# Recurrent attention: the bias of half the heads' decays subtracted on VectorE, their exponentials taken in one instruction

## The reference

```
logfg = log_sigmoid(f_pre); Fcum = cumsum(logfg)
Dmat  = Fcum[s] - Fcum[t] + i_pre[t]          (causal, -inf above the diagonal)
m     = max_t Dmat;  Smat = exp(Dmat - m)
C     = (q k^T / sqrt(dqk)) * Smat
n     = max(|sum_t C|, exp(-m));  h = (C / n) v
```

## Time and profile before

| | |
|---|---|
| median of 3 runs | 699.81 us (698.16 to 700.64) |
| the profiled execution, its own time | 699.76 us |
| its span in the profile | 698.0 us, 12153 instructions |
| TensorE busy | 672.2 us (96%) |
| VectorE busy | 517.6 us (74%) |
| ScalarE busy | 371.4 us (53%) |
| GpSimd busy | 131.0 us (19%) |

### The profile page before, as it was taken

How to read it: one execution, slowest core, us unless ns; L and a number is a source line. 1 busy time by engine, 2 the same in 40 slices (tenths; PEclk the granted TensorE clock), 3 DMA queues, 4 the chain that set the end, 5 groups by cost and what they waited for, 6 DMA issues and landing times.

```text
span 698.0 us, 12153 instructions
## 1 busy us (share of the span) xinstructions
PE 672.2 (96%) x4808; PEld 563.1 (81%) x4808; DVE 517.6 (74%) x919; ACT 371.4 (53%) x775; POOL 131.0 (19%) x125
## 2 busy tenths in 40 slices
PE   7998998999999999999999999999899999999997
PEld 7866875778787888878888878887787889889886
DVE  7736678887957576566675575757679998989996
ACT  5886878856634444444353442446565454454541
POOL 7144535410000020000200002000123213203220
PEclk8999999999999999999999999999999999999999
DMA  5088452000100001010001100150000000000000
GB/s 196 5 253 291 118 157 72 2 1 0 63 1 31 0 1 60 3 31 1 1 23 40 31 1 0 51 223 2 0 1 1 0 10 23 1 31 1 1 31 31
DMA packets 24008, 31.27 MB, mean 45 GB/s; under 512 B 1232, under 2 KB 19952, under 8 KB 23184
## 3 DMA queue, kind: packets, MB, share of 16 engines
q1 hardware_dynamic: 23296, 29.18, 13.1%
q10 hardware_dynamic: 656, 1.31, 0.5%
HBM read 28.18 MB, written 2.31 MB: 44 GB/s over the span
## 4 chain that ended last, share of the span: by engine, by line
PE 68%; DVE 20%; ACT 7%; issue 3%; POOL 1%; DMA 1%; DVEq 0%
PE bank L89 21%; PE bank L91 20%; PE bank L90 20%; DVE l_ring_lo L2535 3%; DVE l_ge L2516 2%; DVE l_h L2531 2%; DVE l_o L2539 1%; DVE h_raw L1214 1%; DVE l_h L2488 1%; ACT m_W L703 1%; PE bank L513 1%; DVE h_ring_lo L1219 1%; PE bank L486 1%; PE bank L501 1%; DVE l_oT_lo L2545 1%
## 5 line engine op out<-in xcount | busy, mean ns | idle before, releaser
L1214 DVE TENSOR_TENSOR h_raw<-h_s,bank 128x512 f32<-128x512 f32 x104 | 71.5, 687 | 107.5 <-ACT h_s L1204 93.2
L1204 ACT ACTIVATE h_s<-bank 128x512 f32<-128x512 f32 x104 | 62.2, 598 | 164.0 <-PE bank L91 163.8
L1219 DVE TENSOR_TENSOR h_ring_lo<-h_raw,h_ring_hi 128x512 fp32r<-128x512 f32 x92 | 69.0, 750 | 0.1
L1208 ACT ACTIVATE h_ring_hi<-h_raw 128x512 fp32r<-128x512 f32 x104 | 64.8, 623 | 2.3 <-DVE h_raw L1214 2.3
L90 PE MATMUL bank<-fused_lo,h_ring_hi 128*128 128x256 f32 x208 | 58.4, 281 | 0.0
L2235 ACT ACTIVATE l_s<-bank 128x512 f32<-128x512 f32 x32 | 19.1, 598 | 64.6 <-PE bank L91 64.6
L89 PE MATMUL bank<-l_xT_hi,l_wgu 128*128 128x512 f32 x128 | 51.3, 401 | 0.1
L89 PE MATMUL bank<-f_yT_hi,mlp_hi 128*128 128x512 f32 x128 | 50.7, 396 | 0.2 <-DVE f_yT_lo L1327 0.2
L90 PE MATMUL bank<-l_xT_lo,l_wgu 128*128 128x512 f32 x128 | 50.3, 393 | 0.0
L91 PE MATMUL bank<-l_xT_hi,l_lo 128*128 128x512 f32 x128 | 50.2, 393 | 0.0
L91 PE MATMUL bank<-f_yT_hi,fused_lo 128*128 128x512 f32 x128 | 50.0, 390 | 0.0
(11 more groups left out here) (372 smaller groups left out, 1977.8 us busy)
## 6 DMA issues: line engine op xcount, KB each, us to landing
m_W<-m_scratch SPq DMA_DIRECT2D x16, 512.0 KB, 6.5
fused_raw<-in_fused SPq DMA_DIRECT2D x1, 3584.0 KB, 13.4
res<-in_x SPq DMA_DIRECT2D x4, 512.0 KB, 6.1
fused_raw<-in_fused SPq DMA_DIRECT2D x2, 1024.0 KB, 9.0
f_mask<-expert_weights SPq DMA_DIRECT2D x8, 256.0 KB
l_raw<-in_layer SPq DMA_DIRECT2D x1, 2048.0 KB, 8.8
out_x<-res SPq DMA_DIRECT2D x16, 128.0 KB, 1.9
f_xw<-in_turned_x SPq DMA_DIRECT2D x3, 512.0 KB, 5.8
```

Source lines behind the costliest of these rows:

```text
L1204: self.nc.scalar.activation(self.s[u % 2][r, :], gate[r, :], ACT.Silu).then_inc(self.silu.sem, 1)
L1208: self.nc.scalar.activation(self.unit(i, u)[0], self.product(i, u), ACT.Copy).then_inc(self.hi.sem, 1)
L1214: self.nc.vector.tensor_tensor(out=self.product(i, u), in0=self.s[u % 2][r, :], in1=up[r, :], op=ALU.mult).then_inc(self.hidden.sem, 1)
L1219: self.nc.vector.tensor_tensor(out=lo, in0=self.product(i, u), in1=f32(hi), op=ALU.subtract).then_inc(self.lo.sem, 1)
```

## The change

The bias of four of the eight heads (SHARED = 4, heads 4 to 7) is no longer given to ScalarE. A new step of VectorE, `bias_weights(n)`, subtracts it from the masked tile, in place, 128 x 512 columns in one instruction with the table's columns spread over 128 query tokens, and counts `biased`. ScalarE takes the first four heads as before, then waits for `biased` and takes one exponential over the remaining 512 columns. Sixteen bias_weights are placed in VectorE's list: those of chunks 0 and 1 ahead of the first weigh_q, and from there bias_weights(n+2) to (n+5) each ahead of weigh_scores(n+1) to (n+4). Where `gated_sum` stood, its two parts are called one after the other, and some `if b:` blocks are written twice.

```diff
+    SHARED = H - 4
+    biased = Signal(dve_tables, C, GA)
...
         def weights(n):
...
-            for h in range(H):
-                last = nc.scalar.activation(w[:, h, :], w[:, h, :], ACT.Exp, bias=tg[:, c, b * H + h:b * H + h + 1], scale=-1.0)
-            last.then_inc(weight.sem, 1)
+            for h in range(SHARED):
+                nc.scalar.activation(w[:, h, :], w[:, h, :], ACT.Exp, bias=tg[:, c, b * H + h:b * H + h + 1], scale=-1.0)
+            act.wait_ge(biased.sem, biased.at(b, c + 1))
+            nc.scalar.activation(w[:, SHARED:H, :], w[:, SHARED:H, :], ACT.Exp, scale=-1.0).then_inc(weight.sem, 1)
...
+        def bias_weights(n):
+            if n >= N:
+                return
+            b, c = divmod(n, C)
+            dve.wait_ge(masked.sem, n + 1)
+            w = W[n % RING][:, SHARED:H, :]
+            nc.vector.tensor_tensor(out=w, in0=w, in1=expand(tg[:, c, b * H + SHARED:(b + 1) * H], P), op=ALU.subtract).then_inc(biased.sem, 1)
...
         dve.wait_ge(act_tables, EA_K)
+        bias_weights(0)
+        bias_weights(1)
         weigh_q(0)
         weigh_scores(0)
         for b in range(B - 1):
             n = b * C
             if b:
                 mean_square(b - 1, 1)
+            if b:
                 add(b - 1, 0)
-                gated_sum(b - 1, 1)
+            if b:
+                sum_squares(b - 1, 1)
+            if b:
+                gate(b - 1, 1)
             weigh_q(b + 1)
+            bias_weights(n + 2)
             weigh_scores(n + 1)
             if b:
                 norm(b - 1, 1)
             carry(b, 0)
             if b:
                 low_h(b - 1, 1)
+            bias_weights(n + 3)
             weigh_scores(n + 2)
             carry(b, 1)
             mean_square(b, 0)
             if b:
                 add(b - 1, 1)
-            gated_sum(b, 0)
+            sum_squares(b, 0)
+            gate(b, 0)
+            bias_weights(n + 4)
             weigh_scores(n + 3)
             norm(b, 0)
             carry(b, 2)
             low_h(b, 0)
+            bias_weights(n + 5)
             weigh_scores(n + 4)
             normal_x(b)
         b, n = B - 1, N - C
         mean_square(b - 1, 1)
         add(b - 1, 0)
+        bias_weights(n + 2)
         weigh_scores(n + 1)
         carry(b, 0)
-        gated_sum(b - 1, 1)
+        sum_squares(b - 1, 1)
+        gate(b - 1, 1)
+        bias_weights(n + 3)
         weigh_scores(n + 2)
         norm(b - 1, 1)
         carry(b, 1)
+        bias_weights(n + 4)
         weigh_scores(n + 3)
```

More of the change, by code:

```diff
@@ L994, in mean_square @@
             nc.vector.tensor_reduce(out=den[f][3][:, x], in_=sq[:, some, :].rearrange("p c (h d) -> p (c h) d", d=DV), op=ALU.add, axis=AX.X).then_inc(ms_steps.sem, 1)
-        def gated_sum(b, f):
-            sum_squares(b, f)
-            gate(b, f)
         def sum_squares(b, f):
@@ L1139, in _ @@
         mean_square(b, 1)
-        gated_sum(b, 1)
+        sum_squares(b, 1)
+        gate(b, 1)
         following.split_low(dve, 0, 1)
@@ L1144, in _ @@
         mean_square(b, 2)
-        gated_sum(b, 2)
+        sum_squares(b, 2)
+        gate(b, 2)
         low_h(b, 0)
```

## The result

The changed kernel takes 702.97 us (median of 4 runs, 702.58 to 703.55), the kernel before 699.48 us beside it (698.16 to 700.64). The ratio is 1.0052, with a 95% interval of 1.0038 to 1.0065: slower by some 3.5 us. The profiled execution took 703.55 us, its span is 701.6 us, 3.6 more than before.

The account below looks back on a forecast made before the run. ScalarE was taken to bound some 10 us of the opening, VectorE's list one stretch per batch. 0.5 (A, B) + 0.9 (C) + 2.86 (D) + 0.6 (E) = +4.9 us on 699.76: 704.6, range 700.8 to 707.6.

Parts of the forecast that it names:

- rival 1: At D VectorE comes first, or no mask holds a subtraction: 702.1 to 703.0 us; chance 0.22.
- D: Subtractions of chunks 9 and 13, behind low_h: GpSimd's mask starts first and holds them; +1.43 us each, +2.86 for two.
- A: Opening, chunks 1 to 3: ScalarE's saving against a subtraction held by a mask; -0.5 us, ends 0 and -1.03.
- B: Chunk 5's subtraction, batch 0: it waits for a mask, then normal_x meets the next; +0.5 us together with A.
- Prices: Per chunk: ScalarE saves 0.65 us; VectorE pays 0.60 for a 0.68 subtraction, which ends 0.45 after a running mask.
- C: Subtractions of chunks 6 and 10, between weigh_q and weigh_scores, delay norm: +0.45 us each, +0.9 for two.
- E: Chunk 14's subtraction, before weigh_scores(13), for which TensorE already waits: +0.60 us, ends 0.55 and 0.65.
- Nothing for the rest: Other chunks' subtractions fall where VectorE waits, and ScalarE's saving after 62 us is worth nothing: no cost or gain.
- 2, faster: ScalarE's saving in the opening arrives and VectorE's gaps hold every subtraction: 697.2 to 698.7 us; chance 0.09.
- 3, the clock: Longer TensorE waits at 68, 91 and 115 us bring low-clock stretches, +1.5 to +3.0: 706.1 to 707.6 us; chance 0.11.
- 4, the root locks: GpSimd's root holds VectorE as the mask does, at chunks 4, 8, 12, 15: 6.4 us on top, 711; chance 0.05.
- 5, absorbed: Unseen slack between 120 and 150 us takes 3 us or more of the shift: 700 to 701.9; chance 0.10.

Follow-up runs that it names:

- dve_only: Changed kernel with ScalarE's eight exponentials with bias restored; VectorE's 16 subtractions go into a spare tile nobody reads: 703.47 us, ratio 1.0047 to the kernel before.
- act_only: Changed kernel without VectorE's subtractions and the wait for them; ScalarE's four exponentials and one wide one stay: 699.56 us, ratio 0.9997 to the kernel before.
- tie: Changed kernel with a small VectorE memset ahead of the subtractions of chunks 5, 9 and 13, to delay them: 704.99 us, ratio 1.0084 to the kernel before.
- after_again: The changed kernel, unaltered, run once more for more times and a second profile: 703.12 us, ratio 1.0059 to the kernel before.
- open_only: Changed kernel with only chunks 1, 2 and 3 the new way, all others with eight exponentials: 700.17 us, ratio 1.0003 to the kernel before.
- from_chunk2: Changed kernel with chunks 0 and 1 back to eight exponentials and no subtraction: 703.51 us, ratio 1.0063 to the kernel before.
- move_c_e: Changed kernel with the subtractions of chunks 6 and 10 moved ahead of weigh_q and chunk 14's beside chunk 15's: 703.28 us, ratio 1.0048 to the kernel before.
- move_n5: Changed kernel with the subtractions of chunks 5, 9 and 13 moved from behind low_h to ahead of norm: 700.65 us, ratio 1.0012 to the kernel before.
- after_nx: Changed kernel with normal_x moved ahead of norm: 699.24 us, ratio 0.9996 to the kernel before.
- all_heads: Changed kernel with all eight heads the new way, a subtraction and an exponential of 1024 columns per chunk: 708.01 us, ratio 1.0127 to the kernel before.
- before_nx: Kernel before the change with only normal_x moved ahead of norm: 698.21 us, ratio 0.9980 to the kernel before.

## Why the prediction was right, step by step

**The direction and the time.** Forecast 704.6, measured 702.97 (range 700.8 to 707.6). dve_only and act_only show the reason: the subtractions cost 3.6 us, and ScalarE's saving is 0.3 by the medians, with an interval on both sides of nothing. The time is rival 1's, "VectorE first", 702.1 to 703.0; its chance was 0.22. The forecast itself was D with GpSimd first, and that didn't happen. That 702.97 still lies within the range is in part luck: in the profile of after, D is 1.9 us smaller than forecast, A and B together are 1.0 larger, and the clock gives back 0.5 that I hadn't counted.

**Prices: right, or near.** 0.62 us for the wide exponential and 0.52 to its successor; 0.68 for the subtraction, 0.60 to its successor (89.30 to 89.89, 117.99 to 118.59). For one that finds a mask running I said 0.45 us after the mask's end (0.68 less 0.2 is 0.48); measured are 0.54 in tie and 0.55 at 64.44 of after (the subtraction ends at 65.61, the mask at 65.06 by its row). The prediction's "0.04 to 0.29 us after GpSimd" doesn't fit the row of the four L1040: it ends at 66.48, 1.12 after the mask. Only one of the four was stretched (1.03 us; the median is 0.41).

**A: wrong in its sign and not settled.** I took -0.5; in the profile of after it is +1.1, in that of after_again -1.4. The difference goes with the clock at its lower level for 10.1 or 3.4 us, in the same kernel. With 3.4 us, as in the kernel before, the gain of 1.4 in after_again is more than my end of 1.03. But it isn't what decides the time: by 75 us both are late, by 2.0 and 1.5 us, and open_only, with only the opening changed, is at 1.0003.

**B: the mechanism was right, its victim was not always the one I named.** The subtraction meets the mask (1.17 us), or, if it comes early, normal_x does (2.83). A and B together were to be +0.5; TensorE goes on 1.54 late in after, 0.82 in dve_only (68.65), and not at all in after_again (67.83). But in these last two, and in from_chunk2 (69.04), the clock falls behind the wait: from the add to the next transposes TensorE takes 7.05, 7.01 and 6.99 us, in after 6.00, in before 5.50. That is 1.0 us for the clock in these three; after, move_c_e and tie, with the subtraction in the same place, have no low clock there. This term was the most under-sized: move_n5, which clears this place and D's, wins back some 2.7 us, and D accounts for 1.0 of them.

**C: right in after, not confirmed by the time.** Said +0.9 for two, measured 0.50 and 0.48, with waits of 0.35 and 0.34 ahead of the transposes. Where the clock is low behind the first add, the first of the two waits isn't there, and move_c_e, which removes both, isn't measurably faster than after_again.

**D: the wrong side of a tie.** Said +2.86 for two, measured 0.47 and some 0.5 (1.12 more of lateness between 99.74 and 119.86, less E's 0.60); TensorE's wait for the second add is 1.29 and not 2.1. The step that failed is "I let GpSimd win": the mask did come up first by the record, by 0.02 us, and gave way. tie shows the price I had named, with GpSimd 0.15 us ahead. Wherever a mask's record is ahead of the subtraction's by 0.01 or 0.02 us, in after, after_again, dve_only, from_chunk2, move_c_e, after_nx and all_heads, VectorE wins, so it isn't chance; but no row of before shows it. I should have given the two sides like chances.

**E: right** in after: weigh_scores(13)'s successor is 0.60 later. **Nothing for the rest: right**, as far as the subtraction of 83.31 inside the root and, with the reserve made there, from_chunk2 (chunks 0 and 1) show. The saving of ScalarE after 62 us brings nothing measurable: act_only.

**The rivals.** 2, faster: act_only, with all of the saving and none of the cost, is not measurably faster. 3, the clock: refuted for the profile of after, which has none at 70 or 92 us, and where the last step of the account, from 4.11 to 3.62, is a gain by it; but it came in after_again, another execution of the same kernel. Behind the waits at the adds the clock is low in after_again (2.70 us), act_only (2.98), dve_only (1.91), from_chunk2 (1.79), all_heads (2.48 and 1.80) and tie (2.20), and not behind those of 1.73 us or less. 4, the root locks: refuted, four subtractions of after lie inside roots of 3.28 us and take 0.70 or 0.71. The Trainium skill (SBUF — State Buffer, section "SBUF: two separate sides") lets a GpSimd instruction that reads SBUF hold the shared ports for its whole length. The masks agree with that (1.48 against 0.68 in tie), these roots do not. 5, absorbed: 0.5 of 4.1 us was given back, by the clock.

What stays open: how the 2.7 us of move_n5, less D's 1.0, divide between B's meeting and the low clock that follows it. From the transposes of batch 0 to the add's product TensorE takes 6.83 us in before, 7.29 in after, 7.46 in dve_only, 8.26 in after_again and 6.21 in move_n5. The profiles show both causes, in other shares each time, and no kernel here holds the clock fixed.

## What to carry to other kernels

Work moved off an engine that is ahead brought nothing measurable here, and it cost where it landed on a list that another engine waits for; ask of each copy of the moved instruction what stands behind it in that list. Where two engines share a resource, a few hundredths of a microsecond in a trace don't tell which will hold the other before a run has shown it: price both, and better, move one of them to where its engine waits anyway (move_n5 gave back most of the loss, and the same thought applied to normal_x, without the change, beat both kernels). An earlier start can be lost to the meeting that it causes, and to the lower clock behind the wait, so follow it through to the next instruction that a DMA releases.

## What the runs showed of the hardware

- The lower clock in the opening, between 36 and 49 us, differs between two executions of the same kernel (10.1 us at the lower level in after, 3.4 in after_again) and between variants: none in act_only and before_nx, 3.4 in the kernel before, some 10 in open_only and move_c_e. I found no row that says which it will be. In after_again and act_only nearly all of such a gain was gone by 75 us.
- In a near tie VectorE's subtraction wins though the mask's row begins 0.01 or 0.02 us sooner (mask 1.65 and 1.64 us in after; VectorE wins in six other profiles too), and loses when the mask is 0.15 or 0.16 ahead (subtraction 1.48). At 0.03 it goes either way: in tie the subtraction of 63.41 wins against the mask of 63.38 (0.63 and 1.61 us), in after_nx that of 64.22 loses against the mask of 64.19 (1.59 and 1.09). At 0.04, in move_n5, it loses (47.27 against 47.23, 1.59 us).
- The key scaling, a GpSimd tensor_tensor of 1.06 us, holds a subtraction as the mask does: 1.47 us at 40.01 of after.
- Behind a wait of TensorE of 1.79 to 2.98 us at an add the granted clock fell to between 0.50 and 0.56 (means over 2 us) in all seven cases; behind 1.73 us and less at an add it didn't. At 121 us it is less regular: 1.93 us brought the lower clock in before and none in open_only.
- normal_x, four instructions with one tensor input each, is held as well, and by a row of three GpSimd instructions: 3.68 us for 1.37 of work in act_only.
- GpSimd's root, 3.28 us, holds none of the subtractions that begin inside it (0.70 and 0.71 us, where 0.68 is the median).
